# Weights split once in the first stage of an attention and mixture-of-experts block, with reordered steps, dispatch and ending

## The chip, the cores and the metric

The kernel runs on one core of one Trainium2 chip. The metric is the device time in microseconds (us) of one execution, taken as the median of several. The profile names the engines PE (TensorE), DVE (VectorE), ACT (ScalarE), POOL (GpSimd) and SP (SyncE, which here only issues DMAs). Each engine works through its own list of instructions in order; a wait in the list holds up everything behind it on that engine.

## The reference, cut to what matters

4096 tokens of width 512 (two batches of 2048), 8 experts with hidden width 256, two of them chosen per token, and a shared expert of hidden width 512. All in float32.

```python
x = L0_attn_X                                     # (2, 2048, 512)
# attention part, on h = layernorm(layernorm(x)) * ln_w + ln_b
Q, K, V = split(h @ W_in + b_in)                  # rope on the first half of Q and K
A = sum over tokens of (K / |K|) * V              # one vector per batch
Y = (A[:, None, :] * Q) @ W_out + b_out + layernorm(x)
x = x + layernorm(Y)
# mixture-of-experts part, on xf = layernorm(x)
gates = softmax over the top 2 of xf @ gate_w
routed = sum over the 2 chosen experts e of gate_e * (gelu(xf @ w1[e] + b1[e]) @ w2[e] + b2[e])
shared = gelu(xf @ shared_w1 + shared_b1) @ shared_w2 + shared_b2
x = x + layernorm(routed + shared)
```

## The kernel before, in words

**Two parts.** A product in float32 precision is made of three passes of TensorE: each operand `a` is made into `a_hi` (rounded by ACT, written as float32r) and `a_lo = a - a_hi` (by DVE or POOL), and the product is `hi*hi + hi*lo + lo*hi`. `product` and its like issue three matmuls for each of the 4 blocks of the inner dimension. A weight must thus exist in SBUF as two tiles, `hi` and `lo`.

**Groups.** The 4096 tokens are 8 groups (`NG`) of 512, each of 4 tiles of 128. Everything is one list for each engine, written out by hand; semaphores are the only tie between the lists.

**Stage one (groups `g` 0 to 7).** On PE: `kv(g, j, c)` for 4 tiles `j` and two outputs `c` (K and V), then `turn(g + 1)` (the transposes of the next group's normalised rows, four times four), then `q(g, m)` for 4 blocks. On ACT: for each `j` `norm_k(g, j)` (the sum of squares of K), after `j == 1` also `q_hi_parts(g - 1)`; then `front_split(g + 1)`, which empties the transposes' two PSUM banks (`hb`, L535, and `h_hi`, L540) and so lets `turn(g + 1)` go on; then `bias_q(g)`. On DVE: `k_tile`, `v_tile`, `kv_prod` for each tile, `front_norm(g + 1)` after the second `k_tile`, `q_lo_parts(g - 1)` (L877) after the second `kv_prod`, and at the end `rotate_q(g)` and `front_stats(g + 2)`. On SP: for each group the next x, `store_q(g - 1)` (Q is kept in DRAM, in two parts of 1 MB), the rope tables, and in groups 1 to 4 `copy_expert` (DRAM to DRAM, 512 KB each, the expert weights in the layout wanted later) and in group 5 the shared expert's.

**Steps (`s` 0 to 7).** PE does `attend(s, 0..2)`, `n3_turn(s - 1)`, `attend(s, 3)`, `gate(s - 1)`, and a `fill`: the shared expert for a group already normalised, first its hidden layer (`shared_h`, 48 matmuls) in one step and then its output (`shared_o`) in the next. Before, steps 2 to 7 have fills, for groups 1, 3 and 5; groups 6 and 7 follow after step 7, and groups 0, 2 and 4 (`LATE`) at the end of the kernel. The chain that leads from `attend(s, 3)` to `n3_turn(s)` is `z_tile`, `z_moments`, `z_rsqrt` (POOL), `x2_tile`, `x2_stats`, `x2_moments`, `x2_rsqrt` (POOL), `x2_shift`, `norm_x2` (ACT). In step 0 POOL and ACT also split the shared weights (`split_s`). The bias `bo` of the attention's output is made ready just before step 0.

**The gap.** After step 7 come the last transposes and gate, the fill for groups 6 and 7, and the making of the lists by which tokens are gathered: DVE counts tokens per expert (from L1089), makes 16 pairs of one-hot matrices (`hot_a`, `hot_q`), and PE turns them into lists (`ids_ps`). Meanwhile the 8 experts' weights come in from DRAM (1 MB each) and `split_expert` (ACT) and `expert_lo` (DVE) make two parts of them (2 MB each).

**Experts.** 72 tiles of 128 rows are gathered, multiplied and scattered with accumulation, a loop that takes from 656 to 909 us.

**Ending.** The three `LATE` groups go through the shared expert (`late_turn`, `late_h`, `late_o`), with its weights loaded and split again (`c_raw`), and every group's final norm is added to the output by a DMA that accumulates.

Of the kernel before, what the change touches and what calls it, by code (L numbers as in the profile page):

```python
# [7 lines left out]
P = 128  # L8
# [11 lines left out]
EARLY = (1, 3, 5, 6, 7)  # L20


def sandwich_kernel(nc, X, ln_w, ln_b, W_in, b_in, W_out, b_out, gate_w, w1, b1, w2, b2,
# [7 lines left out]
    GT = 4  # L31
# [31 lines left out]
    we_dram = dram("expert_scratch", (E, 2, P, KD * H))  # L63
    ws_dram = dram("shared_scratch", (2, P, KD * SH))
# [9 lines left out]
    with ctx:  # L74
# [23 lines left out]
        upper, ones_f = keep("upper", [P, P]), keep("ones_f", [P, P])  # L98
# [43 lines left out]
        wo_lo = [at("wo_lo0", 136, [P, KD, D], F32R), at("wo_lo1", 8, [P, KD, D], F32R)]  # L142
        rc, rsn = at("rc", 144, [P, 2, G]), at("rsn", 148, [P, 2, G])
# [16 lines left out]
        bo_raw, bo_hi = at("bo_raw", 96, [B_ROWS, D]), at("bo_hi", 98, [B_ROWS, D], F32R)  # L160
        bo, bo_one = at("bo", 108, [B_ROWS, D], F32R), at("bo_one", 100, [B_ROWS, P], F32R)
# [11 lines left out]
        zero_d = at("zero_d", 72, [P, D])  # L173
# [32 lines left out]
        c1_hi, c1_lo = at("c1_hi", 96, [P, KD, SH], F32R), at("c1_lo", 104, [P, KD, SH], F32R)  # L206
        c2_hi, c2_lo = at("c2_hi", 112, [P, KS, D], F32R), at("c2_lo", 120, [P, KS, D], F32R)
        c_raw = [at(f"c_raw{i}", kb_, [P, KD, SH]) for i, kb_ in enumerate((136, 164))]
# [10 lines left out]
        rank_ps, ids_ps = bank[2], bank[0]  # L219
        xt_ps, th_ps, h_ps, oe_ps = bank[0:2], (bank[2], bank[7]), bank[3:5], bank[5:7]  # L220
# [10 lines left out]
        fill = {2 + i: (("h", "o")[i % 2], EARLY[i // 2]) for i in range(6)}  # L231
        assert all(fill[s][1] == s - 1 for s in (2, 4, 6))
# [8 lines left out]
        h_order = (1, 3, 5, 6, 7)  # L241
# [23 lines left out]
        measured = beside((0, 0, 0, 0, 1, 1, 1, 1, 2, 2, 2, 2, 1, 1, 0, 0, 2, 2, 1, 1, 0, 0, 0, 0))  # L265
        normed_in = beside((0, 0, 0, 0, 0, 0, 0, 0, 0, 1, 1, 1, 2, 2, 2, 2, 1, 1, 1, 1, 2, 1, 1, 1))
# [16 lines left out]
        f_loads = (EARLY[0], LATE[0], EARLY[1], EARLY[2], LATE[1], EARLY[3], LATE[2], EARLY[4])  # L283


        w_order = (3, 4, 0, 5, 1, 2, 6, 7)
# [10 lines left out]
        we_copied, ws_copied = sem("we_copied"), sem("ws_copied")  # L297
# [22 lines left out]
        s_in, s_hi_done, s_split = [sem(f"s_in{i}") for i in range(2)], sem("s_hi_done"), sem("s_split")  # L320
# [6 lines left out]
        we_in, we_hi_done, we_split = [sem(f"we_in{i}") for i in range(E)], sem("we_hi_done"), sem("we_split")  # L327
# [10 lines left out]
        c_split = sem("c_split")  # L338
        n3c_in, f_in = [sem(f"n3c_in{i}") for i in range(len(LATE))], [sem(f"f_in{i}") for i in range(NG // 2)]
# [9 lines left out]
        def _(sp):  # L349
# [30 lines left out]
            sp.dma_start(sb2_rows[:, :], sb2.partition_broadcast(E)).then_inc(rows_in, 16)  # L380
            sp.dma_start(gw[:, :, :], gate_w.rearrange("(k p) e -> p k e", p=P)).then_inc(late_in, 16)
# [7 lines left out]
            def copy_expert(e):  # L389
                sp.dma_start(we_dram[e, 0].rearrange("p (k h) -> p k h", k=KD), w1[e].rearrange("(k p) h -> p k h", p=P))\  # L390
                  .then_inc(we_copied, 16)
                sp.dma_start(we_dram[e, 1].rearrange("p (k d) -> p k d", k=KH), w2[e].rearrange("(k p) d -> p k d", p=P))\
                  .then_inc(we_copied, 16)
# [5 lines left out]

            for g in range(NG):  # L400
# [12 lines left out]
                if g == 5:  # L413
                    for i, w in enumerate((sw1, sw2)):
                        sp.dma_start(ws_dram[i].rearrange("p (k h) -> p k h", k=KD), w.rearrange("(k p) h -> p k h", p=P))\
                          .then_inc(ws_copied, 16)
# [6 lines left out]
            def load_s(i, lo):  # L423
                sp.dma_start(lo[:, :, :].rearrange("p k h -> p (k h)").bitcast(F32), ws_dram[i]).then_inc(s_in[i], 16)

            sp.wait_ge(tp_full, KD * NG)
            sp.dma_start(bo_raw[:, :], b_out.partition_broadcast(B_ROWS)).then_inc(bo_in, 16)
# [4 lines left out]
            sp.wait_ge(ws_copied, 32)  # L432
            load_s(1, s2_lo)
            store_q(NG - 1)
            sp.wait_ge(q_stored[1], 32 * NG // 2)
            load_q(1)
            load_s(0, s1_lo)
# [6 lines left out]
            for s in range(NG):  # L444
# [3 lines left out]
                if s == 2:  # L448
                    sp.wait_ge(consts_set, F_ZERO)
                    for g in LATE:  # L450
                        sp.dma_start(f_groups[g], zero_d[:, :].rearrange("p (o d) -> p o d", o=1).to_broadcast([P, GT, D]))\
                          .then_inc(zero_stored, 16)
                    sp.dma_start(f_dram[N:N + 4 * P, :].rearrange("(t p) d -> p t d", p=P),
                                 zero_d[:, :].rearrange("p (o d) -> p o d", o=1).to_broadcast([P, 4, D])).then_inc(zero_stored, 16)
                late = [fill[s][1]] if s in fill and fill[s][0] == "o" else []
# [15 lines left out]
            def load_expert(e):  # L471
                for i in range(2):
                    sp.dma_start(we[:, e, 2 * i + 1, :].bitcast(F32), we_dram[e, i]).then_inc(we_in[e], 16)

            s = NG - 1
            sp.wait_ge(we_copied, 16 * 2 * E)
            sp.wait_ge(zero_stored, 16 * (len(LATE) + 1))
            load_expert(3)
            load_expert(4)
# [14 lines left out]
            load_expert(6)  # L494
# [4 lines left out]
            for j in range(GT):  # L499
                store_f(7, j)  # L500
            sp.wait_ge(o_full, NO)
            sp.wait_ge(b2_stored, 16)
            sp.wait_ge(f_stored[0], 16 * f_buf_uses[0])
            sp.dma_start(b2b[:, :, :].rearrange("p e d -> p (e d)"), b2_dram.rearrange("e d -> (e d)").partition_broadcast(P))\
              .then_inc(bias_in[1], 16)

            sp.wait_ge(dst_ready, 1)
            sp.dma_start(n3c[0][:, :, :], n3_groups[LATE[0]]).then_inc(n3c_in[0], 16)
            sp.dma_start(c_raw[0][:, :, :].rearrange("p k h -> p (k h)"), ws_dram[0]).then_inc(s_in[0], 16)
# [4 lines left out]
            for n, g in enumerate(f_loads):  # L514
                sp.dma_start(f[g][:, :, :], f_groups[g]).then_inc(f_in[n // 2], 16)
# [3 lines left out]
        def _(act):  # L519
# [59 lines left out]

            act.sem_inc(tp_free, 2)  # L580
# [5 lines left out]
            for n in range(2 * KD, 3 * KD):  # L586
                hi_part(n)
            act.wait_ge(consts_in, 32)

            for g in range(NG):  # L590
                for j in range(GT):
                    norm_k(g, j)
                    if j == 1 and g >= 1:
                        q_hi_parts(g - 1)
                if g + 1 < NG:
                    front_split(g + 1, (g + 1) % 2)
                    bias_q(g)
                if g == GB:
                    keep_acol(0)
                    scale_wo(0)  # L600
# [4 lines left out]
            act.wait_ge(bo_in, 16)  # L605
            act.activation(bo_hi[:, :], bo_raw[:, :], ACT.Copy).then_inc(bo_hi_done, 1)
            act.wait_ge(bo_set, 1)
            act.activation(bo[0:1, :], bo_raw[0:1, :], ACT.Copy).then_inc(bo_split, 1)
# [22 lines left out]
            def split_s(i, hi, lo):  # L631
                act.wait_ge(s_in[i], 16)
                for h in range(2):
                    s = slice(2 * h, 2 * h + 2)
                    act.activation(hi[:, s, :], lo[:, s, :].bitcast(F32), ACT.Copy).then_inc(s_hi_done, 1)

# [15 lines left out]
            for s in range(NG):  # L652
                if s == 0:
                    split_s(1, s2_hi, s2_lo)
                    split_s(0, s1_hi, s1_lo)
# [8 lines left out]
                if s == NG - 1:  # L664
                    gelu(6, 0)
                    gelu(6, 1)
# [4 lines left out]
            def split_expert(e):  # L671
                act.wait_ge(we_in[e], 32)
                for i in range(2):
                    act.activation(we[:, e, 2 * i, :], we[:, e, 2 * i + 1, :].bitcast(F32), ACT.Copy).then_inc(we_hi_done, 1)

            gelu(6, 2)
            gelu(6, 3)
            split_expert(3)
            split_expert(4)
            n_hi_parts(NG - 1)  # L680
            keep_logits(NG - 1)
            split_expert(0)
            split_expert(5)
            act.wait_ge(gap_ready, 1)
            act.activation(gd[:, :], gd[:, :], ACT.Exp).then_inc(exp_ready, 1)
            split_expert(1)
            for m in range(KS):
                gelu(7, m)
            split_expert(2)
            act.wait_ge(gates_ready, 1)  # L690
            act.dma_start(gates_out, picked[:, :, :]).then_inc(gates_stored, 16)
            split_expert(6)
            split_expert(7)
# [60 lines left out]
            def nc_hi_part(i, k):  # L754
                act.wait_ge(tc_full, KD * i + k + 1)
                act.activation(nc_hi[:, k, :], tp[k % 2][:, :], ACT.Copy).then_inc(nc_hi_done, 1)
# [9 lines left out]
            act.dma_start(c_raw[1][:, :, :].rearrange("p k h -> p (k h)"), ws_dram[1]).then_inc(s_in[1], 16)  # L766
            for i in range(1, len(LATE)):
                act.dma_start(n3c[i][:, :, :], n3_groups[LATE[i]]).then_inc(n3c_in[i], 16)
# [998 lines left out]
```

## Time and profile before

| what | value |
| --- | --- |
| median of 3 runs | 1028.24 us (1027.85 to 1035.12) |
| the profiled execution's own time | 1027.98 us |
| its span, first to last instruction | 1025.8 us |
| PE busy | 896.8 us (87%) |
| DVE, ACT, POOL busy | 628.3, 442.0, 404.4 us |
| mean granted TensorE clock | 0.95 of full |

Busy time of PE is the first thing to read, and then where in the span the rest lies, since the stages have different limits.

### The profile page before, as it was taken

The page shows a single profiled execution, that of the slowest core. Times are in us where ns is not written, and L with a number is a line of the kernel's source. Part 1 is how long each engine was busy: PE and PEld are TensorE (multiplying, and loading weights), DVE is VectorE, ACT ScalarE, POOL GpSimd, SP SyncE. Part 2 cuts the span into 40 slices and gives each one's busy share as a digit, 9 for nine tenths or more (in the row PEclk, how much of TensorE's full clock was granted, in tenths as well). Part 3 has the DMA queues.
Part 4 walks back from the last instruction along what each step waited for, and adds up shares of the span by engine and source line. Part 5 has one row for each costly group of instructions (what it writes and reads, how often), then busy time and mean ns, then how long its engine had stood idle before and what let it go on. Part 6 is the DMA issues. An engine that isn't in the chain of part 4 may idle for free.

```text
span 1025.8 us, 14729 instructions
## 1 busy us (share of the span) xinstructions
PE 896.8 (87%) x4562; PEld 739.3 (72%) x4562; DVE 628.3 (61%) x1356; ACT 442.0 (43%) x830; POOL 404.4 (39%) x337
## 2 busy tenths in 40 slices
PE   1999999999997699999999748499999999969883
PEld 1877787787785467777778537488988988857662
DVE  5656766676664775656665587366665666655653
ACT  4134233433423124122242645366666666653462
POOL 3356446545631400000000000277677777730464
PEclk9999999999998889999999878799999999989886
DMA  9122644545337568645424650678778878789496
GB/s 314 45 81 105 244 143 161 188 158 200 135 144 306 190 239 312 227 165 215 154 83 169 215 151 32 238 144 149 140 147 163 154 146 149 147 176 350 62 160 107
DMA packets 78074, 174.68 MB, mean 170 GB/s; under 512 B 10841, under 2 KB 19289, under 8 KB 73137
## 3 DMA queue, kind: packets, MB, share of 16 engines
q1 hardware_dynamic: 52096, 124.60, 33.6%
q0 software_dynamic: 20592, 45.96, 25.1%
q10 hardware_dynamic: 5312, 3.18, 1.3%
q8 instruction: 41, 0.67, 0.3%
q14 instruction: 33, 0.26, 0.1%
HBM read 103.68 MB, written 80.53 MB: 180 GB/s over the span
## 4 chain that ended last, share of the span: by engine, by line
PE 70%; DVE 11%; issue 7%; ACT 4%; POOL 3%; DMA 2%; SPq 1%; POOLq 0%; ACTq 0%; DVEq 0%
PE bank L1434 12%; PE bank L1435 12%; PE bank L1436 12%; PE bank L1626 3%; PE bank L1628 3%; PE bank L1627 3%; PE bank L1643 3%; PE bank L1645 3%; PE bank L1644 3%; PE bank L1613 3%; PE bank L1429 3%; POOL out L1413 2%; DVE we L1061 2%; PE bank L1635 2%; ACT hb L535 1%
## 5 line engine op out<-in xcount | busy, mean ns | idle before, releaser
L1385 POOL DMA_INDIRECT f_scratch<-ro,dst x71 | 113.2, 1595 | 48.7 <-SPq L513 23.2
L1377 POOL DMA_INDIRECT xr<-n_scratch,ids x72 | 71.1, 987 | 90.9 <-issue 65.6
L1434 PE MATMUL bank<-wkv_hi,h_hi 128*128 128x512 f32 x256 | 101.1, 395 | 3.8 <-issue 3.8
L1436 PE MATMUL bank<-wkv_hi,h_lo 128*128 128x512 f32 x256 | 100.7, 393 | 0.0
L1435 PE MATMUL bank<-wkv_lo,h_hi 128*128 128x512 f32 x256 | 100.6, 393 | 0.0
L1188 DVE TENSOR_TENSOR ro<-bank,b2b 128x512 f32<-128x512 f32 x71 | 49.1, 692 | 70.3 <-PE bank L1645 70.3
L1626 PE MATMUL bank<-we,x_hi 128*128 x284 | 86.4, 304 | 0.0
L1628 PE MATMUL bank<-we,x_lo 128*128 x284 | 80.7, 284 | 0.0
L1627 PE MATMUL bank<-we,x_hi 128*128 x284 | 80.6, 284 | 0.0
L544 ACT ACTIVATE sq<-kb 128x512 f32<-128x512 f32 x32 | 20.3, 633 | 134.2 <-DVE kb L845 134.2
L1344 POOL TENSOR_TENSOR zr<-zv,half 128x4 f32<-128x4 f32 x8 | 8.1, 1009 | 137.7 <-DVE zv L961 137.7
L1296 POOL TENSOR_TENSOR rn<-ssq,half 128x1 f32<-128x1 f32 x32 | 23.4, 731 | 96.2 <-ACT sq L544 96.2
L1434 PEld LDWEIGHTS bank<-wkv_hi,h_hi 128*128 128x128 f32 x256 | 48.7, 190 | 14.3 <-issue 4.2
L1643 PE MATMUL bank<-we,g_hi 128*128 x142 | 56.6, 399 | 1.2 <-DVE g_lo L1180 1.2
L1168 DVE TENSOR_TENSOR x_lo<-bank,x_hi 128x512 fp32r<-128x512 f32 x72 | 49.7, 690 | 11.4 <-ACT x_hi L704 9.9
L1645 PE MATMUL bank<-we,g_lo 128*128 x142 | 56.4, 397 | 0.0
L1435 PEld LDWEIGHTS bank<-wkv_lo,h_hi 128*128 128x128 f32 x256 | 48.8, 191 | 10.2
L1644 PE MATMUL bank<-we,g_hi 128*128 x142 | 56.1, 395 | 0.0
L1436 PEld LDWEIGHTS bank<-wkv_hi,h_lo 128*128 128x128 f32 x256 | 48.6, 190 | 10.3
L1626 PEld LDWEIGHTS bank<-we,x_hi 128*128 128x128 f32 x284 | 54.3, 191 | 0.3 <-issue 0.3
L1434 PE MATMUL bank<-wo_hi,q_hi 128*128 128x512 f32 x128 | 54.3, 424 | 0.0
L1627 PEld LDWEIGHTS bank<-we,x_hi 128*128 128x128 f32 x284 | 54.3, 191 | 0.0
(232 smaller groups left out, 2514.2 us busy)
## 6 DMA issues: line engine op xcount, KB each, us to landing
xg<-in_X SPq DMA_DIRECT2D x16, 1024.0 KB, 9.1
q_scratch<-qh SPq DMA_DIRECT2D x8, 1024.0 KB, 3.9
q_scratch<-qb SPq DMA_DIRECT2D x8, 1024.0 KB, 7.1
expert_scratch<-in_w SPq DMA_DIRECT2D x16, 512.0 KB, 7.1
q_hi<-q_scratch SPq DMA_DIRECT2D x8, 1024.0 KB, 4.7
q_lo<-q_scratch SPq DMA_DIRECT2D x8, 1024.0 KB, 6.9
out<-z SPq DMA_DIRECT2D x8, 1024.0 KB, 5.1
n_scratch<-n SPq DMA_DIRECT2D x8, 1024.0 KB, 6.4
```

The source lines that it names most:

```text
L1168: dve.tensor_tensor(x_lo[u][:, :], xt_ps[u][:, :], x_hi[u][:, :].bitcast(F32), ALU.subtract)\
L1377: pool.indirect_dma_start(xr[u][:, :], None, n3_dram, bass.IndirectOffsetOnAxis(ids[:, i:i + 1], 0)).then_inc(row_in[u], 16)
L1385: pool.indirect_dma_start(f_dram, bass.IndirectOffsetOnAxis(dst[:, i:i + 1], 0), ro[i % NRO][:, :], None, compute_op=ALU.add).then_inc(r_s ...
L1434: pe.matmul(dst, hi(k), w_hi(k), start=(k == 0), stop=False)
L1435: pe.matmul(dst, hi(k), w_lo(k), start=False, stop=False)
L1436: last = pe.matmul(dst, lo(k), w_hi(k), start=False, stop=(k == KD - 1 and not more))
L1626: pe.matmul(out_h, x_hi[u][:, s], part_of(e, 0, k, H), start=(k == 0), stop=False)
L1627: pe.matmul(out_h, x_hi[u][:, s], part_of(e, 1, k, H), start=False, stop=False)
L1628: last = pe.matmul(out_h, x_lo[u][:, s], part_of(e, 0, k, H), start=False, stop=(k == KD - 1))
L1643: pe.matmul(oe_ps[u][:, :], g_hi[u][:, s], part_of(e, 2, k, D), start=(k == 0), stop=False)
L1644: pe.matmul(oe_ps[u][:, :], g_hi[u][:, s], part_of(e, 3, k, D), start=False, stop=False)
L1645: last = pe.matmul(oe_ps[u][:, :], g_lo[u][:, s], part_of(e, 2, k, D), start=False, stop=(k == KH - 1))
```

## The change

- **Units.** The weights of all experts (8 times `w1`, `w2`) and of the shared expert (`sw1`, `sw2` in halves) are 20 units of 512 KB. In groups 1 to 5 of stage one, four units a group: `load_unit` brings one into `w_lo[u % 2]`, ACT writes `w_hi` (`unit_hi`, after `norm_k(g, j)`), DVE writes `w_lo` over the raw values (`unit_lo`), and `store_unit` stores both. There are two pairs of buffers; `load_unit(u + 2)` waits on SP until both stores of unit `u` have landed. The copies from DRAM to DRAM are gone.
- Later loads bring both parts (2 MB an expert, 4 MB for the shared one), and `split_expert`, `expert_lo`, `split_s` and the splits of `c_raw` are gone.
- `EARLY` is (0, 2, 4, 6, 7): the fills begin in step 1 and fill every step to 7; groups 1, 3 and 5 are now late. After step 7 remain `shared_o` of 6 and both parts of 7.
- The bias `bo` is made in group 0. The zeros for `f_scratch` (4 MB) are stored in step 0, not step 2. `scale_wo(0)` comes two groups later.
- Step 7 on DVE has no fill between its chain. In the gap `shared_o(7, 0)` and `(7, 1)` come before the one-hot matmuls, and two, not four, between them.
- The ending's transposes use four banks, the loads come in another order, and the next group's transposes are emptied ahead of the final norms.

```diff
-EARLY = (1, 3, 5, 6, 7)
+EARLY = (0, 2, 4, 6, 7)
...
+            def load_unit(u):
+                if u >= len(units):
+                    return
+                if u >= 2:
+                    sp.wait_ge(w_stored[u % 2], 32 * (u // 2))
+                w, k = unit_in(u)
+                sp.dma_start(w_lo[u % 2][:, :].bitcast(F32).rearrange("p (k h) -> p k h", k=k), w).then_inc(raw_w_in[u % 2], 16)
+
+            def store_unit(u):
+                sp.wait_ge(unit_split, u + 1)
+                for c, w in ((0, w_hi), (1, w_lo)):
+                    sp.dma_start(unit_out(u, c), w[u % 2][:, :].bitcast(F32)).then_inc(w_stored[u % 2], 16)
...
             for g in range(NG):
+                u = UG * (g - 1)
+                with_units = 0 <= u < len(units)
                 sp.wait_ge(h_normed, g + 1)
                 load_x(g + 2)
+                if with_units:
+                    store_unit(u)
+                    load_unit(u + 2)
                 if g >= 1:
                     store_q(g - 1)
+                if with_units:
+                    store_unit(u + 1)
+                    load_unit(u + 3)
+                    store_unit(u + 2)
+                    load_unit(u + 4)
                 if g + 1 < NG:
                     sp.wait_ge(k_rotated, GT * (g + 1))
                     load_rt(g + 1)
                     sp.wait_ge(q_rotated, g + 1)
                     load_rf(g + 1)
-                if 1 <= g <= 4:
-                    copy_expert(2 * g - 2)
-                    copy_expert(2 * g - 1)
+                if with_units:
+                    store_unit(u + 3)
+                    load_unit(u + 5)
...
+            def unit_hi(u):
+                act.wait_ge(raw_w_in[u % 2], 16 * (u // 2 + 1))
+                if u >= 2:
+                    act.wait_ge(w_stored[u % 2], 32 * (u // 2))
+                act.activation(w_hi[u % 2][:, :], w_lo[u % 2][:, :].bitcast(F32), ACT.Copy).then_inc(unit_hi_done, 1)
...
@@ ACT, stage one
                     norm_k(g, j)
                     if j == 1 and g >= 1:
                         q_hi_parts(g - 1)
+                    if 0 <= UG * (g - 1) < len(units):
+                        unit_hi(UG * (g - 1) + j)
                 if g + 1 < NG:
                     front_split(g + 1, (g + 1) % 2)
                     bias_q(g)
...
@@ DVE, stage one
                 kv_prod(g, 0)
+                unit_lo(g, 0)
                 v_tile(g, 1)
                 k_tile(g, 2)
                 kv_prod(g, 1)
                 if g >= 1:
                     q_lo_parts(g - 1)
+                unit_lo(g, 1)
                 v_tile(g, 2)
                 k_tile(g, 3)
                 kv_prod(g, 2)
+                unit_lo(g, 2)
                 v_tile(g, 3)
                 kv_prod(g, 3)
+                unit_lo(g, 3)
...
@@ SP, before and in the steps
+            load_s(0, (s1_hi, s1_lo))
+            load_s(1, (s2_hi, s2_lo))
...
-                if s == 2:
+                if s == 0:
                     sp.wait_ge(consts_set, F_ZERO)
...
@@ SP, the gap
             load_expert(3)
-            load_expert(4)
+            load_expert(4, range(0, 2))
             load_expert(0)
             load_expert(5)
             sp.wait_ge(n3_ready, GT * NG)
...
@@ PE, the gap
-            for m in range(KS):
-                shared_h(6, m)
             n3_turn(NG - 1)
...
             for m in range(KS):
                 shared_h(7, m)
+            shared_o(7, 0)
+            shared_o(7, 1)
...
-                if b in (1, 4, 7, 10):
-                    shared_o(7, (b - 1) // 3)
+                if b in (2, 5):
+                    shared_o(7, 2 + (b - 2) // 3)
```

## Rows read from the trace of the kernel before

**Rows 1.** Busy time by stage: start:end, length, engines, clock, DMA share, GB/s
```profile
40.00:330.00 290.00, 275.24 (x1251) 224.69 (x1251) 184.94 (x358) 105.31 (x181) 141.29 (x105) 0.99 0.45 162
...
600.00:620.00 20.00, 4.48 (x21) 3.81 (x19) 19.31 (x35) 11.21 (x22) 0.00 (x0) 0.62 0.44 107
...
910.00:1026.00 116.00, 81.65 (x336) 65.86 (x336) 60.78 (x156) 50.15 (x73) 45.17 (x52) 0.83 0.80 179
```

**Rows 2.** The same view, group 3 of stage one alone
```profile
137.00:173.20 36.20, 35.03 (x161) 28.63 (x161) 23.51 (x48) 12.86 (x22) 18.89 (x14) 1.00 0.50 174
```

**Rows 3.** Timeline of ACT, group 3: start, length, what, [idle before]
```profile
148.17 2.00 ACT L564 ACTIVATE qh<-qb 128x1024 fp32r<-128x1024 f32 x2
...
158.43 0.63 ACT L544 ACTIVATE sq<-kb 128x512 f32<-128x512 f32 x1 [4.74 <-DVE kb L845]
...
159.46 0.78 ACT L535 ACTIVATE hb<-bank,lnb,lnw 128x512 f32<-128x512 f32 x1 [0.30 <-PE bank L1429]
```

**Rows 4.** Timeline of PE, end of group 3's K and V, start of its Q
```profile
158.82 1.03 PE L1429 MATMUL bank<-ident,hn 128*128 128x128 f32 x8
...
162.09 0.48 PE L1434 MATMUL bank<-h_hi,wq_hi 128*128 128x512 f32 x1
```

**Rows 5.** Timeline of DVE, end of group 2 and group 3
```profile
132.42 1.23 DVE L865 TENSOR_TENSOR rc<-qb,rf 128x1024 f32<-128x1024 f32 x1 [7.05 <-ACT qb L553]
...
150.93 0.69 DVE L836 TENSOR_TENSOR kb<-bank,bkv 128x512 f32<-128x512 f32 x1 [0.33 <-PE bank L1436]
...
153.52 2.35 DVE L877 TENSOR_TENSOR qb<-qb,qh 128x1024 f32<-128x1024 f32 x2
...
156.39 0.68 DVE L836 TENSOR_TENSOR kb<-bank,bkv 128x512 f32<-128x512 f32 x1
```

**Rows 6.** DMA issues, 190 to 194 us; size and us from issue to landing
```profile
q_scratch<-qh SPq DMA_DIRECT2D x1, 1024.0 KB, 4.3
q_scratch<-qb SPq DMA_DIRECT2D x1, 1024.0 KB, 7.1
```

**Rows 7.** The rope table's load of 512 KB, issued at 49.8 us into an idle queue
```profile
DMA to landing us min/median/max: 3.8/3.8/3.8
```

**Rows 8.** DMA issues, 550 to 660 us: the store of n3 behind 4 MB of expert loads
```profile
n_scratch<-n SPq DMA_DIRECT2D x1, 1024.0 KB, 9.7
```

**Rows 9.** Timeline of PE, the start of the steps, idle time in brackets
```profile
325.92 0.79 PE L1509 MATMUL bank<-bo,bo_one 64*128 64x512 f32 x1 [6.67 <-DVE bo L935]
359.05 1.97 PE L1429 MATMUL bank<-ident,n 128*128 128x128 f32 x8 [9.86 <-ACT n L628]
```

**Rows 10.** Timeline of DVE, the start of the steps
```profile
322.42 2.74 DVE L884 SCALAR_TENSOR_TENSOR wo_lo<-raw_o,acol,wo_hi 128x512 fp32r<-128x512 f32 x4 [1.55 <-ACT wo_hi L577]
...
342.42 2.34 DVE L966 SCALAR_TENSOR_TENSOR znm<-zmv,zr 128x4 f32<-128x4 f32 x1 [1.14 <-POOL zr L1344]
344.68 3.61 DVE L967 SCALAR_TENSOR_TENSOR z<-z,zr,xg 128x512 f32<-128x512 f32 x2
...
353.74 2.29 DVE L984 SCALAR_TENSOR_TENSOR xnm<-xmv,xr__76 128x4 f32<-128x4 f32 x1 [1.12 <-POOL xr__76 L1349]
```

**Rows 11.** Line L966 in all 8 steps: ns min/median/max
```profile
L966 DVE SCALAR_TENSOR_TENSOR znm<-zmv,zr x8: 151/154/2343, 342.4 to 546.5; 128x4 f32<-128x4 f32 x8
```

**Rows 12.** Timeline of DVE in the gap
```profile
591.85 0.69 DVE L1023 COPY fo<-bank 128x512 f32<-128x512 f32 x1 [2.52 <-DMA f_scratch<-fo]
...
594.72 0.42 DVE L1089 COPY total<-bank 128x256 f32<-128x256 f32 x1
...
606.69 9.17 DVE L1061 TENSOR_TENSOR we<-we 128x1024 fp32r<-128x1024 f32 x8
...
644.81 0.31 DVE L1149 COPY id_c<-bank 128x144 f32<-128x144 f32 x1 [2.01 <-PE bank L1606]
```

**Rows 13.** The chain that ended last, the wait for the first gathered rows
```profile
648.22 8.03 DMA xr<-n_scratch,ids
```

**Rows 14.** Timeline of PE in the ending
```profile
964.62 1.97 PE L1429 MATMUL bank<-ident,n3c 128*128 128x128 f32 x8 [4.40 <-DVE nc_lo L1211]
```

More of the change, by code:

```diff
@@ L142, in sandwich_kernel @@
         wo_lo = [at("wo_lo0", 136, [P, KD, D], F32R), at("wo_lo1", 8, [P, KD, D], F32R)]
+        UW = KD * H
+        UG = 4
+        units = [(e, i, 0) for e in range(E) for i in range(2)] + [(E + i, 0, h) for i in range(2) for h in range(2)]
+        w_lo = [at(f"w_lo{i}", 128 + 4 * i, [P, UW], F32R) for i in range(2)]
+        w_hi = [at(f"w_hi{i}", 136 + 4 * i, [P, UW], F32R) for i in range(2)]
         rc, rsn = at("rc", 144, [P, 2, G]), at("rsn", 148, [P, 2, G])
@@ L228, in t2_use @@
             return (KD + 1) * g + k
-        fill = {2 + i: (("h", "o")[i % 2], EARLY[i // 2]) for i in range(6)}
-        assert all(fill[s][1] == s - 1 for s in (2, 4, 6))
+        fill = {1 + i: (("h", "o")[i % 2], EARLY[i // 2]) for i in range(7)}
+        assert all(fill[s][1] == s - 1 for s in (1, 3, 5, 7))
         o_order = []
@@ L431, in _ @@
             sp.wait_ge(q_rotated, NG)
-            sp.wait_ge(ws_copied, 32)
-            load_s(1, s2_lo)
             store_q(NG - 1)
+            for u in range(2):
+                sp.wait_ge(w_stored[u], 32 * len(units) // 2)
             sp.wait_ge(q_stored[1], 32 * NG // 2)
             load_q(1)
-            load_s(0, s1_lo)
+            load_s(0, (s1_hi, s1_lo))
+            load_s(1, (s2_hi, s2_lo))
             def store_f(g, j):
@@ L498, in _ @@
               .then_inc(bias_in[0], 16)
-            for j in range(GT):
+            for j in range(GT - 1):
                 store_f(7, j)
@@ L587, in _ @@
                 hi_part(n)
+            act.wait_ge(bo_in, 16)
+            act.activation(bo_hi[:, :], bo_raw[:, :], ACT.Copy).then_inc(bo_hi_done, 1)
+            act.wait_ge(bo_set, 1)
+            act.activation(bo[0:1, :], bo_raw[0:1, :], ACT.Copy).then_inc(bo_split, 1)
             act.wait_ge(consts_in, 32)
@@ L599, in _ @@
                     keep_acol(0)
+                if g == GB + 2:
+                    for u in range(2):
+                        act.wait_ge(w_stored[u], 32 * len(units) // 2)
                     scale_wo(0)
@@ L782, in _ @@
                     gelu_c(i, m)
-                for g, j in y_of[what, i, m]:
-                    normed(g, j)
                 if what == "h" and m == KS - 1 and i + 1 < len(LATE):
@@ L787, in _ @@
                         nc_hi_part(i + 1, k)
+                for g, j in y_of[what, i, m]:
+                    normed(g, j)
             normed(*y_order[-1])
@@ L1037, in _ @@
                 z_moments(s)
+                if s == NG - 1:
+                    break
                 fills(0)
@@ L1055, in _ @@
             s = NG - 1
-            def expert_lo(es):
-                for e in es:
-                    for i in range(2):
-                        dve.wait_ge(we_hi_done, 2 * w_order.index(e) + i + 1)
-                        lo = we[:, e, 2 * i + 1, :]
-                        dve.tensor_tensor(lo, lo.bitcast(F32), we[:, e, 2 * i, :].bitcast(F32), ALU.subtract)\
-                           .then_inc(we_split, 1)
-            for m in range(KS):
+            x2_tile(s, 0)
+            x2_tile(s, 1)
+            x2_stats(s, 0)
+            x2_tile(s, 2)
+            x2_stats(s, 1)
+            x2_tile(s, 3)
+            x2_stats(s, 2)
+            x2_stats(s, 3)
+            x2_moments(s)
+            hs_lo_part(6, 0)
+            x2_shift(s)
+            for m in range(1, KS):
                 hs_lo_part(6, m)
+            top2(s - 1)
             dve.memset(zero_q[:, :].bitcast(F32), 0.0)
@@ L1142, in _ @@
                    .then_inc(hot_marked, 1)
-                if b in (4, 7, 10, 13):
-                    f_out(7, (b - 4) // 3)
-                if b == 9:
-                    expert_lo((7,))
+                for j in {2: (0, 1), 5: (2,), 8: (3,)}.get(b, ()):
+                    f_out(7, j)
             dve.wait_ge(ids_full, 1)
@@ L1682, in late_h @@
                         pe.matmul(sp_[m % 2][:, :], c1_hi[:, k, c], nc_lo[:, k, :], start=False, stop=False)
+                    if n == 0:
+                        pe.wait_ge(c_in[1], 16)
+                    for k in range(KD):
                         last = pe.matmul(sp_[m % 2][:, :], c1_lo[:, k, c], nc_hi[:, k, :], start=False, stop=(k == KD - 1))
```

233 lines of the change are left out of this document (100 added, 133 removed).

## Prediction

> **What bounds the kernel now.** First the busy time by stage. In stage one PE is busy 275.2 of 290 us, at a clock of 0.99; the next engine, DVE, has 184.9 [rows 1]. One group takes 36.2 us, with 144 product matmuls and 16 transposes [rows 2]; without some 3.5 us for the transposes and the waits around them that is (36.2 - 3.5) / 144 = 0.227 us a matmul. So stage one is PE's, and whatever makes PE wait in it lengthens the kernel by as much. The gap is the opposite: from 600 to 620 us PE has 4.48 us of work and DVE 19.31 [rows 1]; DVE's list sets the end. The ending has 81.65 us of PE work in 116 [rows 1]. Second, I read the lists of a group against each other in the timelines, since the change puts work and waits into all of them.
>
> **Stage one: the edit that costs.** A group starts on PE at about 137.1 us, has its K and V done at 158.8, and then `turn(4)` needs ACT: ACT's first `hb` runs at 159.46, 0.30 us after the transposes, and Q begins at 162.09 [rows 3, 4]. ACT must thus be free at 159.5. The change puts four `unit_hi` ahead of it, each 1.00 us (two of this size take 2.00 [rows 3]), and on DVE four `unit_lo` of 1.18 us (two take 2.35 [rows 5]), 4.7 us a group. DVE idles 7.05 us in each group, but ahead of `rotate_q`, behind all this [rows 5]; from 147 to 161 it runs nearly without a break.
>
> (a) DVE alone. Before the last `k_tile` (156.39) come two `unit_lo`; the idle 0.33 us takes in a bit [rows 5]. So it moves to 158.4, K is rotated at 160.4, and ACT does `norm_k(3, 3)` (0.8) and `unit_hi` (1.0): `hb` at 162.3 to 162.7 rather than 159.46. That is 3 us a group even if every unit is there on time.
>
> (b) The units are not on time. There are two pairs of buffers and four units a group. The fourth unit, `u + 3`, uses the buffer of `u + 1`. In this group's times: `unit_lo(g, 1)` stands behind `q_lo_parts`, which began at 153.52 and takes 2.35 [rows 5]; with one `unit_lo` ahead (+1.2, less 0.3) it ends at 156.8, and `unit_lo(g, 1)` ends at 158.0. `store_unit(u + 1)` is issued at 158.1. Ahead of it in SP's queue are the 2 MB of `store_q`, issued at 156.8; these land 7.5 us after their issue (the second is issued 0.4 later and takes 7.1, the first took 4.3 [rows 6]), so at 164.3. The unit's own 1 MB takes 7.5 - 4.3 = 3.2 us more, and the load of `u + 2`, issued just ahead, some 1 us: 168.5. Only then SP issues `load_unit(u + 3)`; 512 KB, in rows of 1 KB like the rope table's, land 3.8 us later [rows 7]: 172.3. `unit_hi` 1.0, and ACT is free at 173.4. PE's transposes wait from about 159.5 to 173.4: 13.9 us a group. Behind ACT's wait are `front_split(g + 1)` and `bias_q(g)`, and for these wait `turn(g + 1)`, all of Q, and the next group; nothing else is in PE's list.
>
> (c) The clock. After 9.86 us of idle the eight transposes at 359.05 take 1.97 us, against 1.03 for the eight at 158.82 [rows 4, 9], the lower of the two levels (1.2 GHz against 2.4). I take 1.5 us a group for the restart, an estimate from this doubling over some 3 us of work.
>
> Together 15.4 us in each of the groups 1 to 5: **+77 us**. From below: the stores land in 4.3 us, as a single MB does [rows 6], though DVE's own delay stays: issue 158.1, landed 162.4, loaded 166.2, `hb` at 167.3; 7.8 us a group, **+39**. From above: the load takes 2.5 us longer beside other traffic and the restart 3 us: 20 a group, **+100**. I take 77 because the queue shows: the store of n3, issued when 4 MB of loads lay ahead, took 9.7 us to land [rows 8], against 4.3 [rows 6].
> The Trainium skill ("DMA: Bandwidth & Descriptors", "Queues, rings and completion order") says that descriptors of one issuing engine are consumed in ring order on each DMA engine, though they may complete otherwise. By that rule the sum is the 77 above; if stores shared the bandwidth evenly it would be nearer 60. The 9.7 us [rows 8] agrees with the rule.
>
> Edits with one answer in stage one: the copies from DRAM to DRAM are gone, and nobody waits for them but the loads much later: 0. The bias in group 0 puts a `bo_set` wait ahead of `norm_k(0, 0)` on ACT and two small operations on DVE, about 1.2 us of delay, with PE's K and V of two tiles still covered by four banks: 0, at most +3. `scale_wo(0)` in group 6 costs ACT 2.6 us before it is needed: 0.
>
> **Start of the steps.** PE waits 6.67 us for `bo` and later 9.86 us for n3 [rows 9]. The first wait is gone, but DVE is busy until 325.2 with `wo_lo_parts(1)` [rows 10] and can take no `z_tile` before 326.5, so step 0's fourth tile is done at about 332.3, not 340.7. From there to the transposes it took 18.4 us (340.7 to 359.05). In it POOL's `split_s` ran beside DVE: `znm` took 2.34 us where 0.154 is the median [rows 10, 11], the shift 2.29, two `x2_tile` 3.61 rather than some 1.4. Without `split_s` 6.4 us go: 12.0. The transposes start at 344.3: -14.7. Against it: the queue of SP now holds 4 MB of shared weights and 4 MB of zeros here; at 3.2 us a MB [rows 6] x for step 2 and the store of n3(0) land near 372, and `norm_x2(1)` waits for the latter. I put +4 for it (0 to +8). Net **-11** (-15 to -5).
>
> **Steps.** Step 1 takes the fill `shared_h(0)`: 48 matmuls of 0.227, **+10.9**. Its cover is none: the 9.86 us of idle lie before it in PE's list. Later steps keep one fill each. The same 10.9 us leave the gap, and are counted there.
>
> **Gap.** I line up the end of `attend(7, 3)`, 541.0 us. Now: `gate`, `shared_h(6)`, transposes at 557; with `split_expert` and `expert_lo` gone the marks are ready at about 572 instead of 588. But `f_out(6, 2)` on DVE waits until the store of `f_out(6, 0)` has landed, as it did before for 2.52 us [rows 12], and that store is now issued behind n3's. SP's queue from 549.5: out 1 MB, experts 7, n3 1, expert 1 2, expert 2 2, then the store. 13.25 MB at some 3.1 us end at 592. DVE is back at L1089 at 594, against 594.72 [rows 12]: the transfers eat 17 us of gain. From there `expert_lo` for four experts (9.17 us) and one more in the loop (2.35) are gone; two of the four `shared_o` stand ahead of the one-hot loop, beside DVE's list but on a slow clock. L1089 to `ids_full`, 50.1 us before [rows 12], becomes some 39. **-12** (-5 where PE's clock holds the loop up, -25 where the small store does not queue). First gathered rows: 8.03 us [rows 13], with 2 MB loaded beside them that now come later: **-3.5** (0 to -5).
>
> **Experts:** the same work, 0. **Ending:** the splits of `c_raw` are gone (some 3 us before the first matmul) and four banks take most of the 4.40 us wait of the turn [rows 14], but n3 for the second late group is loaded only after the last scatter: **-6** (-12 to +2).
>
> **Sum.** 77 - 11 + 10.9 - 12 - 3.5 - 6 = +55.4. The profiled execution took 1027.98 us, 0.3 below the median of 1028.24, so both give **1083 us**.
>
> **Rivals.** *Covered reload.* The change is fast if ACT never waits for a unit: loads would have to land by 161. Then only (a) is left or less: 0 to +16 in stage one, 1006 to 1022. It is the case on the other side; it decides if a unit's store and reload take under 3 us together. 4.3 and 3.8 us [rows 6, 7] speak against it, and for it only that both are measured beside other traffic. *Short cycle.* Stores overtake `store_q`: 39 to 45 in stage one, 1045 to 1051. For it: two queued stores share 16 engines; against it the 9.7 us [rows 8]. *Open gap.* Stage one as forecast, but the small store lands in 2 to 3 us, and L1089 comes 17 us earlier: 1066. *Longer stall.* 20 us a group and slower start of the steps: 1106 to 1112. For it: each group's lateness also moves the stores of the fourth unit towards the next group's first.
>
> **How the numbers follow.** Forecast 0.50; open gap 0.17; short cycle 0.14; longer stall 0.11; covered reload 0.08, of which half is faster by over 1% and half within 1%. A measurement of this kernel can tell about 1% from no change. The range goes from 1042, just below the short cycle, to 1112, and leaves out the covered reload and some of each end. Faster 0.04, within 1% 0.05, slower 0.91.
>
> **What would show it.** In stage one of the new profile: groups 1 to 5 of about 51 us against 36.2, ACT idle before the fourth `unit_hi` with a DMA named, PE idle some 13 us at the turn's third set of transposes, clock below 0.99; groups 6 and 7 at 36.2. At the start of the steps: no wait for `bo`, `znm` at 0.15 us. In the gap: DVE waiting for a store of `f_scratch` some 17 us. The prediction is wrong if groups 1 to 5 are under 40 us: then the landing times [rows 6, 7] don't hold for the units, and the rest, -22 us, is what is left.

## Result and profile after

The changed kernel takes **1068.05 us** (median of four, 1064.8 to 1069.52) against 1029.28 for the kernel before: 1.0362 times as long, interval 1.0322 to 1.0402. It is slower by 39 us. The execution that was profiled took 1064.8 us, with a span of 1063.0 and a clock of 0.937 of full.

First the busy time by stage, to be read against [rows 1, 2]. Columns: start:end, length, then busy time of PE, PEld, DVE, ACT, POOL, the granted clock, the DMA share and GB/s. The stretch of [rows 1] runs to 330, 14 us into the steps. To the end of its stage one the kernel before has

```profile
40.00:316.10 276.10, 268.01 (x1229) 219.44 (x1229) 176.42 (x345) 97.44 (x169) 141.29 (x105) 1.00 0.44 155
```

and the changed kernel, with one group of stage one as the second stretch,

```profile
40.00:383.00 343.00, 275.53 (x1218) 225.93 (x1216) 202.51 (x362) 116.35 (x187) 149.59 (x105) 0.90 0.51 187
87.50:137.00 49.50, 36.66 (x160) 30.12 (x160) 28.70 (x52) 16.79 (x27) 20.66 (x14) 0.86 0.58 212
```

The matmuls are the same, and the stretch is 67 us longer: PE is busy for 275.5 us instead of 268.0, since its clock was 0.90 and not 1.00, and the other 59 are idle. A group of 36.2 us is now one of 49.5: 1.6 us of that is PE's own busy time, which grew from 35.03 to 36.66 at a clock of 0.86, and 11.7 are further idle time. The timeline of PE has them in one piece, where the third set of four transposes needs a PSUM bank that ACT has yet to empty:

```profile
84.65 1.03 PE L1449 MATMUL bank<-ident,hn 128*128 128x128 f32 x8
98.36 1.11 PE L1449 MATMUL bank<-ident,hn 128*128 128x128 f32 x4 [12.67 <-ACT hb L585]
...
400.52 0.79 PE L1454 MATMUL bank<-wo_hi,q_hi 128*128 128x512 f32 x1 [3.67 <-DMA q_lo<-q_scratch]
...
413.30 1.09 PE L1449 MATMUL bank<-ident,n 128*128 128x128 f32 x8
...
697.18 1.09 PE L1635 MATMUL bank<-ident,xr 128*128 128x128 f32 x4 [5.53 <-DMA xr<-n_scratch,ids]
...
981.51 1.97 PE L1449 MATMUL bank<-ident,n3c 128*128 128x128 f32 x16 [3.57 <-DMA n3c<-n_scratch]
```

The same wait stands in groups 1 to 5: 12.67, 12.59, 12.93, 12.56 and 12.59 us; in the groups of before it was 0.43 (and 0.73 at the fourth set). ACT shows why it is late. The `unit_hi` ahead of `hb` waited 8.67 us for a load:

```profile
84.76 1.06 ACT L634 ACTIVATE w_hi<-w_lo 128x1024 fp32r<-128x1024 f32 x1 [4.52 <-DMA w_lo<-in_w]
87.19 0.63 ACT L594 ACTIVATE sq<-kb 128x512 f32<-128x512 f32 x1 [1.37 <-DVE kb L870]
...
96.58 1.06 ACT L634 ACTIVATE w_hi<-w_lo 128x1024 fp32r<-128x1024 f32 x1 [8.67 <-DMA w_lo<-in_w]
97.54 0.76 ACT L585 ACTIVATE hb<-bank,lnb,lnw 128x512 f32<-128x512 f32 x1
```

And SP's list shows what the load waited for:

```profile
82.44 0.32 SPq L422 DMA_DIRECT2D q_scratch<-qh  x1
82.80 0.43 SPq L422 DMA_DIRECT2D q_scratch<-qb  x1
84.66 0.32 SPq L417 DMA_DIRECT2D expert_scratch<-w_hi  x1
85.03 1.25 SPq L417 DMA_DIRECT2D expert_scratch<-w_lo  x1
92.34 0.38 SPq L412 DMA_DIRECT2D w_lo<-in_w  x1
```

The 2 MB of Q go ahead; the unit's stores, issued at 84.66 and 85.03, land 7.3 us after the second of them. The four land in the order of their issue, at 87.2, 89.8, 91.1 and 92.3. Only then is the load issued, and it lands in 4.2 us. Load, `unit_hi`, `hb`, transposes follow one another without a break.

In the gap DVE waits 10.96 us for the small store, with the marks ready at about 641; the lists (L1187) wait for PE:

```profile
632.63 0.69 DVE L1060 COPY fo<-bank 128x512 f32<-128x512 f32 x1 [3.29 <-PE bank L1456]
...
652.69 1.31 DVE L1060 COPY fo<-bank 128x512 f32<-128x512 f32 x2 [10.96 <-DMA f_scratch<-fo]
653.91 0.41 DVE L1128 COPY total<-bank 128x256 f32<-128x256 f32 x1
...
691.69 0.31 DVE L1187 COPY id_c<-bank 128x144 f32<-128x144 f32 x1 [2.57 <-PE bank L1628]
```

SP's list shows that this store is late twice over:

```profile
621.23 1.77 SPq L518 DMA_DIRECT2D n_scratch<-n  x1
623.10 18.67 SPq L510 DMA_DIRECT2D we<-expert_scratch  x2
641.81 0.98 SPq L476 DMA_DIRECT2D f_scratch<-fo  x2
```

DVE had filled `fo` at 633.3, but SP issues the store at 641.81. Its list stood at expert 2's load, which waits until the store of n3 has landed, and that took 20.1 us behind 7 MB of expert loads. The small store then takes 10.9 us more, behind the loads of the experts 1 and 2.

Between marks that both kernels have, the lengths are, in us (the marks are starts or ends of named instructions in the timelines, and "step 7" is its last `z_tile`; "again" is the pair of runs at the end of the next section):

| stretch | before | after | difference | difference again | forecast |
| --- | --- | --- | --- | --- | --- |
| start to end of stage one | 316.1 | 383.2 | +67.1 | +70.2 | +77 |
| to the last `z_tile` of step 7 | 224.9 | 222.7 | -2.2 | -1.0 | -0.1 |
| to DVE's `total` | 53.7 | 48.0 | -5.7 | -5.8 | -0.7 |
| to DVE's `id_c` | 50.1 | 37.8 | -12.3 | -12.3 | -11.3 |
| to the first expert matmul | 12.5 | 8.2 | -4.3 | -3.7 | -3.5 |
| loop of the experts | 252.2 | 257.4 | +5.2 | 0.0 | 0 |
| ending | 116.3 | 105.7 | -10.6 | -12.1 | -6 |
| span | 1025.8 | 1063.0 | +37.2 | +35.3 | +55.4 |

So outside stage one the change does save: 30 to 35 us. Stage one costs twice that.

### The profile page after: what moved, and what is told of

It reads as the page before. It is cut to its first block, busy times and chain, and to the rows that moved or that the text cites. A ratio compares the mean times of both kernels' runs of the same rounds, so it can differ in the third digit from the quotient of the medians.

```text
span 1063.0 us, 14784 instructions
## 1 busy us (share of the span) xinstructions
PE 904.6 (85%) x4562; PEld 742.0 (70%) x4562; DVE 625.5 (59%) x1355; ACT 438.0 (41%) x826; POOL 403.1 (38%) x333
## 4 chain that ended last, share of the span: by engine, by line
PE 54%; DVE 14%; DMA 13%; issue 6%; ACT 6%; SPq 3%; POOL 2%; POOLq 0%; DVEq 0%; ACTq 0%
PE bank L1454 9%; PE bank L1455 9%; PE bank L1456 9%; DMA n_scratch<-n 3%; PE bank L1650 3%; PE bank L1635 3%; PE bank L1648 3%; PE bank L1649 3%; DMA expert_scratch<-w_lo 3%; PE bank L1667 2%; PE bank L1666 2%; PE bank L1665 2%; PE bank L1657 2%; DMA f_scratch<-ro,dst 2%; DMA w_lo<-in_w 2%
## 5 line engine op out<-in xcount | busy, mean ns | idle before, releaser
L1449 PE MATMUL bank<-ident,hn 128*128 128x128 f32 x128 | 25.2, 344 | 83.8 <-ACT hb L585 70.2
L1449 PEld LDWEIGHTS bank<-ident,hn 128*128 128x128 f32 x128 | 18.4, 174 | 89.6 <-ACT hb L585 75.2
L1327 POOL TENSOR_TENSOR rn<-ssq,half 128x1 f32<-128x1 f32 x32 | 27.6, 861 | 105.5 <-ACT sq L594 105.5
L1322 POOL TENSOR_TENSOR h_lo<-hb,h_hi 128x512 fp32r<-128x512 f32 x32 | 40.9, 1281 | 43.5 <-ACT h_hi L590 42.8
```

## Experiments

Experiments 1 to 4 shared one chip, 5 to 8 a second, 9 and 10 a third, each with runs of the kernel before; a ratio is always to those. Where only one execution was made, the reading is in its trace.

**1. The fourth unit off the path.** ACT makes `unit_hi(u + 3)` after `bias_q(g)`, and DVE `unit_lo(g, 3)` after `rotate_q(g)`. All work is there, and the same loads and stores.

```diff
-                    if 0 <= UG * (g - 1) < len(units):
+                    if j < 3 and 0 <= UG * (g - 1) < len(units):
                         unit_hi(UG * (g - 1) + j)
                 if g + 1 < NG:
                     front_split(g + 1, (g + 1) % 2)
                     bias_q(g)
+                if 0 <= UG * (g - 1) < len(units):
+                    unit_hi(UG * (g - 1) + 3)
...
-                unit_lo(g, 3)
                 rotate_q(g)
+                unit_lo(g, 3)
```

> ACT makes each group's fourth unit after bias_q, and DVE its low part after rotate_q; the same work, transfers and buffers, only that nothing of PE's waits behind ACT's wait for that unit's load. Theory of the stall (ACT's in-order list holds the turn's transposes): the groups 1 to 5 of stage one fall from 49.5-50.7 us to 38 to 39.5 (the rest is DVE's and ACT's own extra work ahead of the last K tile), PE's five idle stretches of 12.6 us fall under 3 us, and the kernel's time is 1010 to 1018 us, below the kernel before. Rival, that the stage is slowed by the traffic or by the added work itself wherever it stands: groups stay over 45 us and the time over 1045.

Measured: 1021.04 us, ratio 0.9917 (0.9897 to 0.9936). PE's wait at the turn falls from 12.6 us to 2.95, 3.17, 3.17, 3.17 and 2.94, and stage one ends at 336.4 rather than 383.2. That is 47 us from the place of one wait in two lists. The time is above the range that I gave, by 3 us: from turn to turn it is 40.2 to 41.7 us rather than 38 to 39.5, and three of the five waits are not under 3.

**2. No stores of units.** `store_unit` only raises the semaphore; the scratch is filled later with copies of the weights.

```diff
-                for c, w in ((0, w_hi), (1, w_lo)):
-                    sp.dma_start(unit_out(u, c), w[u % 2][:, :].bitcast(F32)).then_inc(w_stored[u % 2], 16)
+                sp.sem_inc(w_stored[u % 2], 32)
...
+                if g in (5, 6):
+                    for v in range(10 * (g - 5), 10 * (g - 4)):
+                        w, k = unit_in(v)
+                        for c in range(2):
+                            sp.dma_start(unit_out(v, c).rearrange("p (k h) -> p k h", k=k), w).then_inc(filled, 16)
```

> The units are made but not stored in groups 1 to 5 (the scratch is filled with unsplit copies in groups 5 and 6, so the experts' and the shared expert's results differ from the reference); the fourth unit's load is issued as soon as the second is made. Theory of the stall, with the stores' landing (7.7 us after issue, behind store_q) as its larger part: PE's idle stretch at the turn falls from 12.6 us to 3 to 5 us in groups 1 to 4. Rival, that the load itself or the ACT and DVE work is the larger part: it stays over 8 us.

Measured: the wait is 7.29, 7.24, 7.27, 7.25 and 7.29 us, not the 3 to 5 that I expected. The load of the fourth unit is issued at 86.47, right behind `store_q`'s 2 MB (84.17 and 84.55), and takes 6.5 us to land, against 4.2. With the store away the 2 MB hold up the load itself. The total (1069.36) says nothing of this, for the late copies cost 27 us elsewhere:

```profile
383.88 0.79 PE L1459 MATMUL bank<-wo_hi,q_hi 128*128 128x512 f32 x1 [27.01 <-DMA q_lo<-q_scratch]
```

**3. Q stored behind the unit.** Same work, one call moved on SP.

```diff
-                if g >= 1:
-                    store_q(g - 1)
                 if with_units:
                     store_unit(u + 1)
                     load_unit(u + 3)
+                if g >= 1:
+                    store_q(g - 1)
+                if with_units:
                     store_unit(u + 2)
```

> SP issues store_q of the group before behind the second unit's stores and the fourth unit's load, instead of ahead of them; nothing else changes. If the queue is served in order (2 MB ahead of the unit's 1 MB), the unit's stores land 4 to 5 us after issue instead of 7.7 and the idle stretch falls from 12.6 to 8.5 to 10 us, the time to 1045 to 1055 us. If transfers share the engines evenly, little changes: over 11.5 us, 1060 to 1068.

Measured: 1049.47 us, ratio 1.0194 (1.0174 to 1.0214). The waits are 8.91, 9.01, 9.52, 9.06 and 9.08 us. The unit's stores now land 2.6 and 3.6 us after their issue, and SP's list shows the cycle shortened by that:

```profile
85.49 0.32 SPq L417 DMA_DIRECT2D expert_scratch<-w_hi  x1
85.85 0.43 SPq L417 DMA_DIRECT2D expert_scratch<-w_lo  x1
89.43 0.38 SPq L412 DMA_DIRECT2D w_lo<-in_w  x1
89.86 0.47 SPq L422 DMA_DIRECT2D q_scratch<-qh  x1
```

From issue to landing 3.6 us behind nothing, 7.3 behind 2 MB issued 2 us earlier: what is issued later waits behind what was issued first. By the Trainium skill ("DMA: Bandwidth & Descriptors", "Queues, rings and completion order") the descriptors of one issuing engine are taken in ring order on each DMA engine. These two times agree, and so do the four landings in the changed kernel, 87.2 to 92.3, in the order of issue.

**4. The small store first.** In the gap SP stores `f_out(6, 0)` ahead of expert 5's load, and `f_out(6, 1)` ahead of experts 1 and 2.

```diff
             load_expert(0)
-            load_expert(5)
             sp.wait_ge(n3_ready, GT * NG)
             sp.dma_start(n3_groups[s], n3[:, :, :]).then_inc(n3_stored, 16)
+            store_f(6, 0)
+            load_expert(5)
+            store_f(6, 1)
```

> In the gap, SP issues the first store of f before expert 5's load and the second before those of experts 1 and 2, not behind all; same transfers. Theory that DVE's 10.96 us wait for that store (behind some 8 MB of expert loads) sets the gap: the wait is gone or under 3 us, the copy of the counts comes 7 to 10 us earlier after attend(7, 3), and the time falls by 6 to 10 us, to 1058 to 1062. Rival, that the loads of the last experts then become late or PE sets the gap: no gain, 1065 to 1070.

Measured: 1061.37 us, ratio 1.032 (1.0299 to 1.0341). From step 7 to `total` it is 38.5 us rather than 48.0, with 1.62 us of wait left:

```profile
641.95 1.28 DVE L1062 COPY fo<-bank 128x512 f32<-128x512 f32 x2
644.85 0.69 DVE L1062 COPY fo<-bank 128x512 f32<-128x512 f32 x1 [1.62 <-DMA f_scratch<-fo]
645.45 0.41 DVE L1130 COPY total<-bank 128x256 f32<-128x256 f32 x1
```

The part behind it grows by 2.0 us (39.8 against 37.8), so 7.5 us are won: DVE's list was held by a 256 KB store behind expert loads. Without them the store takes 3.0 us, from 634.25, and the second 2.2, the 2 to 3 us of the rival *open gap*. The edit also puts n3's store ahead of expert 5's load (it lands after 14.4 us, not 20.1), so the two causes of the lateness, SP's wait for n3 and the queue, were not taken apart.

**5. Neither the unit's stores nor Q's ahead of the load.** Experiment 2 with the move of experiment 3. What the scratch holds, and so what the later parts multiply, are copies of the weights that were not split.

> As e2 (units made, not stored; unsplit copies fill the scratch in groups 5 and 6, so results differ from the reference), and store_q of the group before also goes behind the fourth unit's load. In e2 the idle stretch fell from 12.6 to 7.25 us only. If the rest of it is the load's wait behind the 2 MB of store_q, it falls to 3 to 4.5 us here, the size that DVE's and ACT's own work and a load of 4 us give. If a load itself takes that long in company, it stays at 6 to 7.5.

Measured: waits of 5.06, 4.88, 4.87, 5.13 and 5.05 us, a little over the range. The last load is issued at 85.8 and lands in 4.2. This is the floor of the cycle with the fourth unit in its place: DVE's own lateness, a load, and `unit_hi`.

The variants thus take the 12.6 us apart: 5.0 are left with no store ahead of the load; the unit's own store adds 4.0 (9.0 in experiment 3); the 2 MB ahead of it add 3.6. The shares depend on the order: without the unit's store the 2 MB cost 2.2 (experiment 2 against 5).

**6. Experiments 1 and 4 together**, with both edits as above.

> Fourth unit behind bias_q and rotate_q (e1) and the small stores of f early in the gap (e4) together. The two places are 200 us apart, so the gains should add: 1021.0 less 7 to 9.5 gives 1011 to 1014 us, ratio 0.982 to 0.985. If one hides the other, 1018 to 1022.

Measured: 1008.56 us, ratio 0.9826 (0.9805 to 0.9847). The ratio is as expected, and the two gains add; the time is 2.4 us under the range, on a chip where the kernel before took 1025.85 instead of 1030.12.

**7. The second unit's `unit_lo` later too.** Experiment 6, and on DVE

```diff
                 if g >= 1:
                     q_lo_parts(g - 1)
-                unit_lo(g, 1)
                 v_tile(g, 2)
                 k_tile(g, 3)
                 kv_prod(g, 2)
+                unit_lo(g, 1)
                 unit_lo(g, 2)
```

> e6, and DVE makes the second unit's low part after kv_prod(g, 2), not before the last K tile. The stretch that is left at the turn (3.0 us in groups 1 to 4, against 0.7 before) is put down to two units' low parts (1.2 us each) ahead of the last K tile; one moved behind takes 1.2 us from it: 1.7 to 2.1 us a group, 5 to 6 us less in all, 1006 to 1009. Rival: its store is then later, the fourth unit's load comes after bias_q and holds up the next group: no gain or a loss.

Measured: **1000.36 us**, ratio 0.9754 (0.9738 to 0.9771), 8 us under experiment 6 where I expected the last `k_tile` to move by 1.2 us a group and little more, 1006 to 1009. In its old place this `unit_lo` took 2.30 us, beside POOL's `acc`, and in the new one 1.2. Two groups of lines of PE, the turn and Q of group 1, first in experiment 6 and then here, tell where the rest comes from (columns: count, busy us, mean ns of one, idle before):

```profile
L1458 PE MATMUL bank<-h_hi,wq_hi 128*128 128x512 f32 x15 | 6.9, 463 | 0.0
...
L1453 PE MATMUL bank<-ident,hn 128*128 128x128 f32 x8 | 1.8, 360 | 3.7 <-ACT hb L587 3.7
```
```profile
L1458 PE MATMUL bank<-h_hi,wq_hi 128*128 128x512 f32 x16 | 6.4, 402 | 1.0 <-ACT qb L605 1.0
...
L1453 PE MATMUL bank<-ident,hn 128*128 128x128 f32 x8 | 1.3, 286 | 2.2 <-ACT hb L587 2.2
```

PE's waits at the third set of transposes sum to 8.9 us over the five groups (1.44, 1.68, 2.54, 1.70, 1.56) where they were 15.4, and 3.2 us of waits for `qb` come up in their place: 3.3 us. Stage one ends 8.3 us earlier (327.9 against 336.2), so some 5 us are the clock's; PE's busy time from 40 us to the end of the stage agrees, 269.4 instead of 274.7. After 2.94 us of waiting it was at the lower level for part of Q, whose `h_hi` matmuls took 463 ns in the mean; after 1.44 us it stayed at the higher, 402. In experiment 6 they took 421 to 463 in all five groups; here 402 in the groups 1, 3 and 5, and 428 and 442 in the other two, though the longest wait, 2.54 us, stands before Q with 402. A single one takes 0.63 us at the lower level and 0.39 at the higher.

**8. Loads of the ending not held back.** The loop of the experts was 257.4 us in the changed kernel's trace and 252.2 in that of before, with single tiles of 3.8 to 4.5 us among those of 3.48. My theory was that the ending's first loads fall into the loop; here, in experiment 6, they are let go before it:

```diff
             sp.wait_ge(dst_ready, 1)
-            sp.wait_ge(xt_full, 2 * NX)
             load_n3(0)
```

> e6, and the two loads of 1 MB for the ending (n3 of the first late group, c1) go out at once when the lists are ready, as in the kernel before, not after eight tiles. In all kernels with the change the expert loop takes 257 to 259 us against 252.2. If these loads in the loop, or the loop's earlier start against its gathers, make it so, the loop falls to 252 to 254 here and the way from the lists to the first expert matmul rises from 8.3 to 12 us. If not, the loop stays at 257 and more.

Measured: the loop takes 254.4 us, but in experiment 6 itself it is 252.9, so there was nothing left to explain, and the loads now hurt the first gathered rows (a wait of 9.06 us, against 5.67). 1011.95 us. The theory falls: the same loop behind the same lists took 257.0 us in experiment 4 and 252.9 in 6. What differed was the chip, and the edit of experiment 1, which alone had 258.7.

**9 and 10. Both kernels once more, on one chip.** No edit.

> The kernel before, unchanged, profiled beside the next run on one chip. In question is the loop of the experts, from its first to its last matmul: 252.2 us in the first profile of before, 257.4 in that of the changed kernel, 257.0 to 258.6 in four variants measured together on one chip and 251.5 to 254.4 in four variants measured together on another, among them pairs with the same loop and the same lists ahead of it. Theory A, the 5 us come with the chip: then this loop and that of the next run are within 2 us of each other here, both near 252 or both near 257. Theory B, the change lengthens the loop: then 252 here against 257 in the next.

> The changed kernel, unchanged, on the same chip as the run ahead of this. Theory A (the chip sets the 5 us): the loop of the experts within 2 us of the other's. Theory B (the change does): 5 us longer than the other's, about 257. By either, PE idles 12.5 to 13 us at the turn of groups 1 to 5, the end of stage one lies 67 us later than in the other, and the spans differ by 32 us under A and 37 under B.

Measured: spans of 1023.4 and 1058.7 us, and the loop is 252.8 in both. The stretched tiles are not the change's: four variants on one chip had 257.0 to 258.7, four on another 251.5 to 254.4, and these two, on a third, 252.8. What on those chips, or at those times, stretches the tiles stays open. The spans differ by 35.3 us, between my 32 and 37: stage one by 70.2 rather than 67. All other stretches differ as in the first pair (the table above, "again").

## Why the prediction was right, and where it was off

The sign, the place and the mechanism hold. 1068 lies in the range of 1042 to 1112; the forecast of 1083 is 15 us too high, 18 against the profiled execution. By the time alone the rival *open gap* (1066) would be nearer, but its condition isn't met: the small store took 10.9 us and held DVE. By its steps:

- **Stage one, the cycle (b).** Right as a chain: `unit_lo(g, 1)`, its store behind `store_q`, landing, reload, `unit_hi`, `hb`. Experiments 1, 2, 3 and 5 each take out one or two links, and PE's wait gets shorter each time. The size was off: I had the unit's store issued at 158.1 and landed at 168.5, 10.4 us, by adding its own 3.2 us and a load's 1 us to Q's landing. It takes 7.3 from the issue of its second half and 7.7 from that of its first. The reload takes 4.2 where I had 3.8. PE's idle time grew by 11.7 us a group, where I had 13.9; over five groups 11 us, which covers the 7 to 10 by which +67 and +70 miss +77. My +39 from below was too far down: experiment 3 has nothing ahead of the unit's store, and there the waits are 8.9 to 9.5 us where I had 7.8, and stage one is 51 us longer than before. The "short cycle", stores overtaking `store_q`, does not happen.
- **Stage one, DVE alone (a).** 3 us forecast, 2.0 by DVE and 1.0 by the fourth `unit_hi`; PE waits 2.94 to 3.17 in experiment 1, where before it waited 0.43. That the size agrees is partly luck: experiment 1 takes this `unit_hi` away, and `unit_lo(g, 1)` takes 2.30 us where I had 1.18.
- **Stage one, the clock (c).** 1.5 us forecast; busy time grew by 1.6. Experiments 6 and 7 show that part of it is still paid where the wait is only 3 us.
- **Start of the steps.** `n3_turn(0)` comes 30.1 us after the end of stage one against 42.95 [rows 9]: -12.9, where I had -14.7. The wait for `bo` is gone, `znm` takes 0.155 us where it took 2.34 [rows 10, 11], PE waits once more for `q_lo` (3.67). The +4 for the full queue did not appear: -12.9 and the fill's +10.9 make -2.0, and -2.2 was measured (-1.0 in the pair). The Trainium skill ("SBUF — State Buffer", "SBUF: two separate sides") has a DVE operation with two SBUF inputs and a GpSimd operation that reads SBUF take one port pair as an exclusive lock. The 2.34 us of `znm` (inputs `zmv` and `zr`) beside POOL's `split_s`, and 0.155 without it, agree.
- **Gap, up to `total`.** The wait for a small store behind the experts' loads is there (10.96 us; I had 17, with the marks ready 31 us after step 7, and they were at 35), and experiment 4 confirms its cause, though not how much of it is SP's wait for n3's store, which my sum by bytes did not name. I had DVE at `total` 53 us after step 7; it took 48.0. The queue began 1.3 us earlier than forecast, and from its first issue at 613.1 to the landing at 652.7 it needed 39.6 us for the 13.25 MB for which I had 42.5. With a gain already of 5.7 us, "the transfers eat 17 us" was too much by 5.
- **Gap, lists and first rows.** -12.3 against -11.3, and -4.3 or -3.7 against -3.5: right.
- **Experts.** 0 forecast and 0.0 in the pair on one chip, so the +5.2 of the first pair is not the change's.
- **Ending.** -10.6 and -12.1 against -6. n3 for the second late group does come late (3.57 us), as foreseen. To PE's last matmul the ending takes 92.0 us instead of 98.8; what I had left out is what follows it, 13.7 us instead of 17.6 (in the pair on one chip 90.1 instead of 98.6, and 13.8 instead of 17.3). In the timelines POOL issues five last additions to the output from 1011.18 on before, taking 4.44 us, and two from 1053.36 after, taking 1.76. That reading was not tested apart.

The sum is +35 to +37 instead of +55.4: 7 to 10 us from stage one, 5 from the gap up to `total`, 1 to 2 behind it, 5 to 6 from the ending, 1 to 2 from the steps, all to the same side; in the first pair the loop gave 5 back.

## What to carry to other kernels

When work is put into the idle time of an engine that works in order, look at what stands behind its wait: here a unit whose own result nobody needed for 95 us (the shared expert's) to over 200 (the others') held `hb` and with it PE, five times, and moving it two calls down turned a loss of 3.6% into a gain of 0.8%. Work out a buffer's whole cycle (last reader, store, what is queued ahead of the store, landing, reload) and put the consumer behind its end; and let small stores that someone waits for go ahead of large loads that nobody waits for yet. When stages differ in what limits them, take the ledger stage by stage: this change was worth 30 us and more everywhere but in the one stage in which it was paid for, and the best of the variants (1000.36 us) keeps it all.

## What the runs showed of the hardware that was not expected

- Waits of PE of only 2.94 to 3.17 us, once in a group, were followed by part of Q at the lower clock (421 to 463 ns in the mean, in five groups of five). With waits of 1.44 to 2.54 us it was two groups of five, and not those with the longest wait.
- The loop of the experts took 257.0 to 258.7 us in four variants on one chip, 251.5 to 254.4 in four on another and 252.8 twice on a third, while none of the edits touches it but that of experiment 8. A difference of 5 us in a stretch that a change does not touch has to be measured on one chip before it is explained.
- Alone, `unit_lo` takes 1.22 us; at 82.33, while POOL ran `acc` (L1334, 1.90 us instead of 1.26), it took 2.30, and the second unit of each of the groups 2 to 5 took 2.30 or 2.31 too:

```profile
82.33 2.30 DVE L908 TENSOR_TENSOR w_lo<-w_lo,w_hi 128x1024 fp32r<-128x1024 f32 x1
...
87.74 1.22 DVE L908 TENSOR_TENSOR w_lo<-w_lo,w_hi 128x1024 fp32r<-128x1024 f32 x1
```
